# Attention divided after transfers inside SBUF instead of after TensorE transposes, repeated products formed once, and a new instruction order

## The reference

```
h = layernorm(layernorm(x)) * ln_w + ln_b
q, k = rope(h @ w_q), rope(h @ w_k);  v = h @ w_v          # 16 heads of 16
s = 0.25 * (q_h . k_h);  t = 1 + s + 0.5 * s * s           # taylor softmax
attn = t / (sum of t over the rows of k)
x = x + layernorm((attn @ v) @ w_o)
z = layernorm(x)
x = x + layernorm(fp6_blocks(z) @ fp6_blocks(weight).T + bias)
```

## Time and profile before

| | us |
|---|---|
| median of 3 runs | 669.49 (669.19 to 670.33) |
| profiled execution, its own time | 669.42 |
| its span | 667.4 |
| TensorE busy | 654.2 |
| VectorE busy | 607.4 |
| ScalarE busy | 565.2 |
| GpSimd busy | 409.6 |

### The profile page before, as it was taken

The page is one execution under the profiler, slowest core; times in us unless marked ns, Lnnn a source line. Parts: engine busy times, 40 slices in busy tenths (PEclk is TensorE's granted clock), DMA queues, the critical chain, the costliest instruction groups (busy, mean ns, idle before and its releaser), DMA issues.

```text
span 667.4 us, 20456 instructions
## 1 busy us (share of the span) xinstructions
PE 654.2 (98%) x6712; PEld 499.2 (75%) x6712; DVE 607.4 (91%) x1522; ACT 565.2 (85%) x1547; POOL 409.6 (61%) x722
## 2 busy tenths in 40 slices
PE   7789999999999999999999999999999999999999
PEld 6676767787777778777777877787777778777678
DVE  6889888999999999999999999999999999896797
ACT  4478989899898989889898988989898888889974
POOL 3557455677756665775666577566657766653465
PEclk9899999999999999999999999999999999999999
DMA  7100000111111011111101111110201101011101
GB/s 238 33 3 32 2 33 2 33 42 49 50 49 42 17 52 47 42 49 50 49 10 56 42 42 49 49 49 10 68 31 41 49 19 50 9 31 36 65 26 55
DMA packets 28165, 28.34 MB, mean 42 GB/s; under 512 B 1824, under 2 KB 27936, under 8 KB 28064
## 3 DMA queue, kind: packets, MB, share of 16 engines
q1 hardware_dynamic: 27248, 26.26, 12.3%
q10 hardware_dynamic: 816, 0.79, 0.4%
HBM read 18.65 MB, written 8.39 MB: 41 GB/s over the span
## 4 chain that ended last, share of the span: by engine, by line
PE 94%; ACT 2%; issue 1%; DVE 1%; DMA 1%; POOL 1%; ACTq 0%; POOLq 0%; DVEq 0%
PE ps_f L627 13%; PE ps_mt L801 12%; PE ps_o L679 8%; PE ps_o L682 8%; PE ps_qk L583 5%; PE ps_qk L586 5%; PE ps_qk L584 5%; PE ps_w L583 4%; PE ps_w L586 4%; PE ps_w L584 4%; PE ps_tr L650 4%; PE ps_o L716 4%; PE ps_tr L583 2%; PE ps_tr L584 2%; PE ps_tr L586 2%; PE ps_tr L664 2%
## 5 line engine op out<-in xcount | busy, mean ns | idle before, releaser
L942 ACT ACTIVATE feat<-ps_f 128x512 f32<-128x512 f32 x256 | 153.9, 605 | 1.1 <-PE ps_f L627 0.9
L627 PE MATMUL ps_f<-qT,selr 128*128 128x512 f32 x320 | 143.4, 450 | 0.0
L519 DVE TENSOR_TENSOR kf<-kf 128x768 f32<-128x768 f32 (+1 forms) x128 | 140.3, 1099 | 2.0
L1481 POOL TENSOR_TENSOR qsp<-kf,qsp 128x256 fp32r<-128x256 f32 x64 | 51.9, 811 | 81.8 <-ACT qsp L1040 81.8
L627 PEld LDWEIGHTS ps_f<-qT,selr 128*128 128x128 f32 x320 | 60.1, 188 | 53.8 <-ACT feat L942 45.4
L519 POOL TENSOR_TENSOR kf<-kf 128x256 f32<-128x256 f32 x64 | 89.8, 1404 | 6.6 <-DVE kf L1288 6.6
L801 PE MATMUL ps_mt<-kf,vp 128*32 128x161 f32 x2048 | 83.4, 303 | 1.8 <-ACT kf L1045 1.0
L992 ACT ACTIVATE hT<-ps_tr,small,lnwx 128x128 f32<-128x128 f32 x128 | 51.7, 454 | 34.6 <-PE ps_tr L664 34.6
L801 PEld LDWEIGHTS ps_mt<-kf,vp 128*32 128x32 f32 x2048 | 60.5, 110 | 18.0 <-issue 15.4
L679 PE MATMUL ps_o<-feat,main 128*32 128x512 f32 x512 | 66.9, 594 | 0.5 <-issue 0.5
L682 PE MATMUL ps_o<-feat,rm 128*32 128x512 f32 x512 | 66.7, 592 | 0.0
(11 more groups left out here) (188 smaller groups left out, 1985.4 us busy)
## 6 DMA issues: line engine op xcount, KB each, us to landing
xc<-L_attn_x SPq DMA_DIRECT2D x16, 512.0 KB, 4.0
result<-fin SPq DMA_DIRECT2D x64, 128.0 KB, 1.7
xa<-L_attn_x SPq DMA_DIRECT2D x15, 512.0 KB, 4.1
wkqv<-L_attn_w_kv ACTq DMA_DIRECT2D x2, 256.0 KB, 5.0
xa<-L_attn_x SPq DMA_DIRECT2D x1, 384.0 KB, 6.6
csel<-selection SPq DMA_DIRECT2D x1, 320.0 KB, 6.9
wkqv<-L_attn_w_q ACTq DMA_DIRECT2D x1, 256.0 KB, 4.1
wf<-L_ffn_weight SPq DMA_DIRECT2D x1, 256.0 KB, 6.2
```

What stands on the lines that cost most here:

```text
L519: return eng.tensor_tensor(dims(row, F_MAIN, [[FW, heads], [HD, NR], [1, HD]]), dims(row, F_LIN, [[FW, heads], [0, NR], [1, HD]]), dims(ro ...
L627: pe.matmul(ps_f[i % 2][:, :], selr[:, i], qT[:, par, quad], start=True, stop=True).then_inc(sel_done, 1)
L942: act.activation(feat[:, p2, i], ps_f[i % 2][:, :], ACT.Square).then_inc(squared, 1)
L1481: pool.tensor_tensor(dims(qsp[:, p2], HQ * HD, [[2 * HQ * HD, NQ], [HD, HQ], [1, HD]]), dims(kf[:, p2, 0, 0:1], F_Q, [[HQ * FW, NQ], [FW, ...
```

## The change

For the first 14 sequences (`BODY` = 56 tiles) the transposes of `turn_quads` and `turn_attention` are gone. SyncE moves each quad instead (`move_quad`, 8 transfers): the denominators go to `sums` (64 partitions by 128), and the 16 rows of each head go to `heads_out`, where the heads lie packed. Once for each sequence VectorE inverts `sums` (`invert_sums`), and SyncE spreads each reciprocal over the 16 rows of its head (`spread_shares`, 8 transfers into `shares`, each to 128 partitions from 8). `normalise_attention` multiplies the two tiles, and its result `att` already stands as `project_out` needs it. The low part is made by GpSimd. The last two sequences keep the old way. The products of opposite pairs (distance 8) were formed twice; now 8 of them are formed (`half_turn`, GpSimd), and `k_products` makes seven rows of 16 instead of eight. The `squares` tiles have one buffer instead of two. All order tables are new.

```diff
+NP = HD * (HD - 1) // 2
+F_ONE, F_MAIN, F_SQ, F_LIN, F_EXT = 0, 1, 1 + NP, 1 + NP + HD, 1 + NP + 2 * HD
 NF = F_EXT
-F_Q = F_EXT + NR
+F_HALF = F_MAIN + (NR - 1) * HD
+F_Q = F_EXT + NR - 1
...
-    "turn_quads": 11, "turn_z": 0, "rest_matrix": 3, "select_0": 6, "turn_ffn_weight": 4, "fill_b": 0,
...
+    "turn_sums": 3, "ffn": 16, "select_4": 7, "turn_q": 3, "turn_quads": 11, "project_kq": 1,
...
+    "bias_mean": 16, "to_grid": 16, "rest_terms": 4, "weight_result": 8, "products_1": 3, "normalise_attention": 13,
...
+    "invert_sums": 9, "add_ffn": 18, "scales": 15, "invert_denominators": 12,
...
         def k_products(eng, t, first, heads):
             row = kf[:, t.two, first, 0:1]
-            return eng.tensor_tensor(dims(row, F_MAIN, [[FW, heads], [HD, NR], [1, HD]]),
-                                     dims(row, F_LIN, [[FW, heads], [0, NR], [1, HD]]),
-                                     dims(row, F_LIN + 1, [[FW, heads], [1, NR], [1, HD]]), ALU.mult)
+            return eng.tensor_tensor(dims(row, F_MAIN, [[FW, heads], [HD, NR - 1], [1, HD]]),
+                                     dims(row, F_LIN, [[FW, heads], [0, NR - 1], [1, HD]]),
+                                     dims(row, F_LIN + 1, [[FW, heads], [1, NR - 1], [1, HD]]), ALU.mult)
...
+            def move_quad(t):
+                par, quad, s = t.par, t.tile, t.seq
+                if t.n > BODY:
+                    return
+                if quad == 0:
+                    wait(sp, norm_ready, NT * (s - 1))
+                    wait(sp, shares_in, 16 * CH * NT * s)
+                sp.wait_ge(o_copied, t.n)
+                for part in range(NT):
+                    sp.dma_start(sums[part * H + HQ * quad:part * H + HQ * (quad + 1)],
+                                 osb[HD:P:VW, par, quad, part * P:(part + 1) * P]).then_inc(sums_in, 16)
+                for h in range(HQ):
+                    row = HD * (HQ * (quad % 2) + h)
+                    sp.dma_start(heads_out[row:row + HD, par, quad // 2], osb[VW * h:VW * h + HD, par, quad]).then_inc(heads_in[par], 16)
+            def spread_shares(t):
+                s = t.seq
+                if t.n > BODY:
+                    return
+                wait(sp, norm_ready, NT * s)
+                sp.wait_ge(inverted, s + 1)
+                for tile in range(NT):
+                    for c in range(CH):
+                        first = tile * H + c * HC
+                        sp.dma_start(shares[:, c, tile * P:(tile + 1) * P],
+                                     dims(sums[first:first + HC, 0:1], 0, [[0, HD], [1, P]])).then_inc(shares_in, 16)
             load_stream(1)
             load_again(0)
@@ -671,12 +728,10 @@
...
                 wait(pe, o_copied, issued["attend"])
-                wait(pe, norm_ready, min(issued["turn_quads"], TILES - NT * 2))
-                wait(pe, aT_low, min(issued["turn_attention"], TILES - NT * 2))
...
             def turn_attention(t):
+                if t.n <= BODY:
+                    return
...
             def turn_quads(t):
                 tile, par = t.tile, t.par
+                if t.n <= BODY:
+                    return
...
+                pe.wait_ge(half_ready, t.n)
...
             def high_attention(t):
-                act.wait_ge(aT_done, t.n)
+                if t.n > BODY:
+                    act.wait_ge(aT_done, t.n - BODY)
+                else:
+                    act.wait_ge(norm_ready, t.n)
                 wait(act, wo_done, t.n - 2)
-                act.activation(attT_h[:, t.two].rearrange("p c n -> p (c n)"), out_bank(t)[:, 0:D], ACT.Copy).then_inc(aT_high, 1)
+                source = out_bank(t)[:, 0:D] if t.n > BODY else att[:, t.two]
+                act.activation(attT_h[:, t.two].rearrange("p c n -> p (c n)"), source, ACT.Copy).then_inc(aT_high, 1)
...
-                wait(act, ot_done, NT * (t.seq - 1))
+                wait(act, sums_in, 16 * NQ * NT * (t.seq - 1))
+                wait(act, heads_in[par], 16 * H * (t.load - 1))
...
+                wait(act, y_squared, t.n - 1)
+                act.activation(squares["y"][:], ps_w[:, 0:D], ACT.Square, scale=ROOT,
                                accum_out=var["y"][:, t.two:t.two + 1]).then_inc(y_squared, 1)
...
+            def invert_sums(t):
+                if t.n > BODY:
+                    return
+                dve.wait_ge(sums_in, 16 * NQ * NT * (t.seq + 1))
+                dve.reciprocal(sums[:], sums[:]).then_inc(inverted, 1)
             def invert_denominators(t):
-                dve.wait_ge(ot_done, t.n)
+                if t.n <= BODY:
+                    return
+                dve.wait_ge(ot_done, t.n - BODY)
                 wait(dve, norm_ready, t.n - 1)
                 dve.reciprocal(rden[:], by_head(t)[:, :, HD]).then_inc(rden_done, 1)
             def normalise_attention(t):
-                dve.wait_ge(rden_done, t.n)
-                wait(dve, aT_done, t.n - 2)
+                low_attention_done(dve, t.n - 2)
+                if t.n <= BODY:
+                    dve.wait_ge(heads_in[t.par], 16 * H * t.load)
+                    dve.wait_ge(shares_in, 16 * CH * NT * (t.seq + 1))
+                    part = slice(t.tile * P, (t.tile + 1) * P)
+                    dve.tensor_tensor(att[:, t.two].rearrange("p (c n) -> p c n", c=CH), heads_out[:, t.par, :, part],
+                                      shares[:, :, part], ALU.mult).then_inc(norm_ready, 1)
+                    return
+                dve.wait_ge(rden_done, t.n - BODY)
                 dve.tensor_tensor(att[:, t.two].rearrange("p (h d) -> p h d", d=HD), by_head(t)[:, :, 0:HD],
                                   dims(rden[:], 0, [[1, H], [0, HD]]), ALU.mult).then_inc(norm_ready, 1)
-            def low_attention(t):
+            def low_attention_late(t):
+                if t.n <= BODY:
+                    return
                 dve.wait_ge(aT_high, t.n)
                 wait(dve, wo_done, t.n - 2)
...
+            def half_turn(t):
+                pool.wait_ge(rope_ready, t.n)
+                row = kf[:, t.two, 0, 0:1]
+                pool.tensor_tensor(dims(row, F_HALF, [[FW, H], [1, NR]]), dims(row, F_LIN, [[FW, H], [1, NR]]),
+                                   dims(row, F_LIN + NR, [[FW, H], [1, NR]]), ALU.mult).then_inc(half_ready, 1)
+            def low_attention(t):
+                if t.n > BODY:
+                    return
+                pool.wait_ge(aT_high, t.n)
+                wait(pool, wo_done, t.n - 2)
+                pool.tensor_tensor(attT_l[:, t.two].rearrange("p c n -> p (c n)"), att[:, t.two],
+                                   attT_h[:, t.two].rearrange("p c n -> p (c n)").bitcast(F32), ALU.subtract).then_inc(aT_low, 1)
```

More of the change, by code:

```diff
@@ L87 @@
+    "add_x": 1, "scale_ln": -20, "add_f": 18, "rstd_x": 1, "tables": -19, "rstd_s": 16, "low_attention": 14,
+    "rstd_f": 18, "half_turn": 3, "products_2": 3, "low_q": 3, "add_y": 14, "low_h": 1, "rstd_y": 14, "add_s": 15,
+    "move_quad": 9,
 }
 FIRST = {
[L90 to L92 removed]
@@ L414, in sandwich @@
         osb = sb("osb", [P, 2, NQ, T])
+        csel = dims(osb[:, 0, 0, 0:1], 0, [[1, CHUNKS * P]])
+        heads_out = sb("heads_out", [P, 2, CH, T])
+        shares = sb("shares", [P, CH, T])
+        sums = sb("sums", [HEADROWS, P])
         rden = sb("rden", [P, H])
@@ L555, in step @@
             def step(n):
+                each(n, "move_quad", move_quad)
+                once(n, "invert_sums", spread_shares)
                 each(n, "add_ffn", store)
@@ L850, in step @@
                 each(n, "turn_ffn_input", turn_ffn_input)
-                each(n, "sum_features", sum_features)
+                each(n, "turn_attention", turn_attention)
+                once(n, "rest_matrix", rest_matrix)
+                each(n, "attend", attend)
+                late(n, "drain_b", drain)
+                early(n, "fill_a", fill)
+                late(n, "drain_a", drain)
+                each(n, "sum_features", sum_features)
+                each(n, "select_2", select, 2)
+                setup(n, "turn_ffn_weight", turn_ffn_weight)
+                each(n, "project_v", project_v)
+                early(n, "fill_b", fill)
+                each(n, "select_3", select, 3)
+                once(n, "turn_sums", turn_sums)
+                each(n, "ffn", ffn)
+                each(n, "select_4", select, 4)
+                each(n, "turn_q", turn_q)
+                each(n, "turn_quads", turn_quads)
+                each(n, "project_kq", project_kq)
             every_step(step)
@@ new lines, in step @@
+                setup(n, "low_kq", low_kq)
+                setup(n, "bias_mean", bias_mean)
+                each(n, "to_grid", to_grid)
+                once(n, "rest_terms", rest_terms)
+                setup(n, "weight_result", weight_result)
+                each(n, "products_1", products, 1)
+                each(n, "normalise_attention", normalise_attention)
+                each(n, "from_grid", from_grid)
```

(12 more changed lines are left out.)

456 lines of the change are left out of this document (214 added, 242 removed).

## The result

The changed kernel takes 691.58 us (median of four runs, 689.65 to 693.26), against 669.60 for the kernel before on the same chip. The ratio is 1.0326, with an interval of 1.0294 to 1.0359: it is slower by 22 us, where 633 us was forecast, and it lies outside the range of 622 to 666.

The account below looks back on a forecast made before the run. The prediction took TensorE, busy 654.2 of 667.4 us, to bound the kernel: 669.42 less 40.8 us of TensorE work gives 628.6, plus 4.4 for VectorE's and ScalarE's tighter pace makes 633 us, range 622 to 666.

Parts of the forecast that it names:

- the sum: Whole kernel: profiled time 669.42 less TensorE's 40.8 us gives 628.6 us, if TensorE stays full.
- TensorE's part: TensorE's list: transposes gone from 56 tiles, 37.0 us, and fewer columns in `sum_features`, 3.8 us; together 40.8 us less.
- The pace: VectorE at 97% and ScalarE at 96% leave TensorE less room: 4.4 us added, bounds nothing to 15 us.
- Start and end are priced as they are: Program's start and end: no change charged; last 8 tiles keep the old way, load-to-store lag stays 18 steps.
- seven gaps of 0.47 and a store's 1.7 us to landing make 5.0 us: SyncE's eight spreads after the inversion: time from first issue to last landing, 5.0 us.
- cover of 5.25: VectorE's twelve instructions between inversion and first `normalise_attention`: 5.25 us in which the spreads must land.
- Late shares would first use up VectorE's 1.1 us; each further microsecond costs 14: Price of late spreads at `normalise_attention`: VectorE's spare 1.1 us a sequence absorbs first, then 14 us per microsecond.
- The one of half the engines: Rival: spreads run on eight engines at 48 ns a packet, landing after 7.5 us; 649 us, chance 0.17.
- The slow one: Rival: spreads' packets obstruct each other in the same eight partitions; at 72 ns, 10.5 us landing, 691 us; chance 0.16.
- VectorE's pace: Rival: VectorE sets the pace and its present waits stay, 15 us more; 643 us, chance 0.14.
- the gain eaten exactly: Rival: spreads land between 8.8 and 9.05 us, cancelling the gain; 669 us, no change, chance 0.03.
- The small terms: VectorE's reciprocal 1.2 us, its products an eighth less; GpSimd's `half_turn` at most 0.70 us, `low_attention` 0.74 us.

Follow-up runs that it names:

- sixteen rows: The changed kernel with each spread reading 16 rows of `sums`, each copied 8 times, instead of 8 rows 16 times; 674.49 us.
- wait for six: The changed kernel with two semaphores, so that a sequence's first division waits for six of the eight spreads; 652.24 us.

## Why the prediction was wrong

The time divides as follows: 628.6 (the sum) + 8.6 (the middle's pace and the two ends) = 637.2; 637.2 + 37.2 (standstill) + 17.2 (clock) = 691.6.

- **TensorE's part was right in the middle.** The transposes and columns are gone from its list; the columns were worth 3.6 us where 3.8 stood, and without the wait the kernel gains 31.8 of the 40.8 us.
- **The pace was right, the ends were not.** 4.4 us were taken, 8.6 came (637.2 - 628.6), within the bounds of nothing to 15. Ten sequences in the middle, from one `fb` to the same one ten sequences later, before and in the kernel with a semaphore for each tile (busy time of PE, PEld, DVE, ACT, POOL; clock; DMA share; GB/s):

```profile
164.66:552.26 387.60, 387.60 (x4083) 297.42 (x4081) 365.85 (x921) 343.96 (x950) 251.73 (x441) 1.00 0.13 41
162.08:524.45 362.37, 361.18 (x3843) 270.69 (x3841) 355.11 (x852) 341.77 (x952) 304.71 (x521) 1.00 0.28 76
```

  A sequence fell from 38.76 to 36.24 us, and 36.2 were forecast: 0.36 above 35.88, of which 0.12 are idle time of TensorE and 0.24 busy time. That is 3.6 of the 8.6 us. The other 5 lie ahead of these ten sequences and behind them, where the forecast had "Start and end are priced as they are". TensorE's idle time there grew from 13.2 to 16.2 us; the rest of the 5 is open. VectorE was 98% busy where 97 stood, but 35.5 us a sequence where 34.74 stood. That it did not come to matter is no merit of the sum: it had 0.7 us to spare and not 1.1.
- **The step that failed first:** "seven gaps of 0.47 and a store's 1.7 us to landing make 5.0 us", and behind it "So 5.0 us against a cover of 5.25: no wait". The cover was right (5.06), the landing was not: 8.0 us, of which 1.4 us are the gaps (0.67, since the row of the start, was of two loads) and 1.65 the last landing (3.35, since the row was of a store from 128 partitions). Both prices were taken from the cheapest rows at hand, and "no wait, but with nothing to spare" went into the sum as nothing.
- **The step that failed second:** "Late shares would first use up VectorE's 1.1 us; each further microsecond costs 14". By it a landing of 8.0 us and its 3.2 us of wait give 633 + 14 x 2.1 = 662 us. The runs gave two corrections. The idle time that VectorE has over a sequence does not lie where the wait is: only 0.5 us were absorbed, the lead of `fb` over TensorE at that one place. That makes 14 x 0.6 = 8 us more. And the formula had no clock: 17.2 us. With the 4.2 us by which the 8.6 are above the 4.4 this comes to 692, against 691.6 measured.
- **The rivals.** The one of half the engines had the landing nearest to what was seen (7.5 us forecast, 8.0 measured), but by 48 ns a packet; at the measured 33 it gives 128 x 33 ns + 1.3 = 5.5 us. The issues (4.7 us) and the last landing (3.35) made the 8.0, so that the landing came near was luck. It priced it at 649 us, since it used the same second step. The slow one named 691 us, which is the time measured, but for another reason: a landing of 10.5 us and no lower clock. A right number was no proof of it; its 72 ns a packet are refuted by 33, and its reason does not hold in the code, where each spread reads another eight partitions of `sums`. VectorE's pace did not set the time, and no run shows the gain eaten exactly.
- **The small terms.** The reciprocal takes 0.93 us, between its bounds of 0.4 and 1.2. `half_turn` takes 0.80 us, above the bound of 0.70, and `low_attention` on GpSimd 0.85 for 0.74, both hidden. VectorE's products of 672 values take 1.10 us on average, longer than the 0.95 that 768 values took in the earlier trace rows, where the forecast took an eighth off; that is 0.2 to 0.3 us more than forecast, four times a sequence.

What was open in the forecast was told there: the landing time of the shares, for which no row stood. What was not seen is that the wait had been written for all eight, when the first division needs two: 0.67 + 3.35 = 4.0 us, inside the cover of 5.06.

## What to carry to other kernels

A semaphore that counts a batch makes the first consumer wait for the last transfer; give each consumer the count of what it reads, before anything is done about the transfers' speed. When a wait is put into a list that runs in order, price it at the first instruction behind it that the bounding engine needs, by the lead at that instruction, and not by the waiting engine's idle time over a whole stretch. If the bounding engine is TensorE, read the granted clock behind standstills of like length and add it. Here a stretch at the lower clock cost 1.6 us, and 12 of 14 standstills of 2.5 to 3.7 us had one behind them; those of 1.0 to 1.5 us had none, one of 1.89 had. Count the stretches in the trace; the length of the standstill alone does not say.

## What the runs showed of the hardware

- SyncE issued small transfers inside SBUF back to back mostly every 0.64 to 0.67 us, eight mostly in 5.1 to 5.4 us whether the source has 8 rows or 16, and in some sequences up to 6.4 us (8 rows) and 6.5 us (16 rows), against 0.47 for the two loads of the earlier trace rows.
- TensorE's mean granted clock over the middle was 0.96 with standstills of 2.5 to 3.7 us, 0.98 with those of 1.5 to 3.0 us (sixteen rows) and 1.00 with those of 1.0 to 1.9 us (wait for six). Idle products in the gap kept it at 1.00, and were worth 17.2 us.
- VectorE's and GpSimd's products took longer in the new order. In the kernel with the halved products alone, the group of 128x672 reads

```profile
L523 DVE TENSOR_TENSOR kf<-kf 128x672 f32<-128x672 f32 x64 | 55.9, 874 | 0.0
```

  and in the changed kernel 1104 ns, and GpSimd's `qsp` of 128x256 went from 811 ns before to 1025. The Trainium skill, page "SBUF — State Buffer", section "Who interferes with whom", has it that a VectorE instruction with two inputs in SBUF contends with a GpSimd instruction that reads SBUF; the rows agree in direction, and no run here tested the overlap by itself. The forecast had left this out.
